# A mixture-of-experts loop regrouped into pairs of tiles, with six shared-expert units moved inside it

## What is computed

```python
logits = jnp.einsum('btc,ec->bte', x, router_w)          # 16 experts
top_vals, top_idx = jax.lax.top_k(logits, TOP_K)         # TOP_K = 2
gates = jax.nn.sigmoid(top_vals)
...
gu = jnp.einsum('nc,ech->neh', xf, gate_up_w)            # per expert, 128 -> 256
gate, up = jnp.split(gu, 2, axis=-1)
h = jax.nn.silu(gate) * up
out_all = jnp.einsum('neh,ehc->nec', h, down_w)          # per expert, 128 -> 128
moe = jnp.einsum('ne,nec->nc', w_full, out_all)
sg = jnp.einsum('btc,sc->bts', x, shared_gate_w)         # shared expert, for every row
su = jnp.einsum('btc,sc->bts', x, shared_up_w)
shared = jnp.einsum('bts,cs->btc', jax.nn.silu(sg) * su, shared_down_w)
return moe + shared
```

## Time and profile before

| | |
|---|---|
| median of 3 runs | 781.0 us (776.43 to 783.17) |
| the profiled execution, its own time | 782.83 us |
| its span, first to last instruction | 780.8 us |
| PE busy | 591.2 us (76%) |
| DVE busy | 495.7 us (63%) |
| POOL busy | 330.2 us (42%) |
| ACT busy | 288.7 us (37%) |
| mean granted TensorE clock | 0.889 of full |

### The profile page before, as it was taken

How to read it: one execution, slowest core, us unless ns; L and a number is a source line. 1 busy time by engine, 2 the same in 40 slices (tenths; PEclk the granted TensorE clock), 3 DMA queues, 4 the chain that set the end, 5 groups by cost and what they waited for, 6 DMA issues and landing times. The chain is left out here.

```text
span 780.8 us, 17864 instructions
## 1 busy us (share of the span) xinstructions
PE 591.2 (76%) x5275; PEld 392.6 (50%) x5276; DVE 495.7 (63%) x1390; ACT 288.7 (37%) x812; POOL 330.2 (42%) x628
## 2 busy tenths in 40 slices
PE   4775888888888888778778887875667876777772
PEld 3554666566665665344434444453335654655441
DVE  8564677886778766689798888874422332232367
ACT  2523444454444542144333434432223433343110
POOL 7531333323233231116565766765424544454100
PEclk9976999999999998699889889987877897797997
DMA  5785344335433533513231322320222222222343
GB/s 156 119 286 77 77 78 60 73 78 83 68 60 72 79 75 73 135 47 81 62 95 52 96 61 74 82 68 17 91 56 69 75 72 76 67 82 64 122 121 94
DMA packets 95331, 65.85 MB, mean 84 GB/s; under 512 B 24752, under 2 KB 90624, under 8 KB 95296
## 3 DMA queue, kind: packets, MB, share of 16 engines
q1 hardware_dynamic: 90688, 55.44, 31.7%
q0 software_dynamic: 4608, 9.97, 4.0%
HBM read 20.54 MB, written 17.56 MB: 49 GB/s over the span
## 5 line engine op out<-in xcount | busy, mean ns | idle before, releaser
L573 POOL DMA_INDIRECT expert_out<-ey,xt x80 | 77.5, 969 | 91.7 <-DVE ey L878 74.8
L968 ACT ACTIVATE probs<-ps 128x512 f32<-128x512 f32 x128 | 73.1, 596 | 64.0 <-PE ps L1364 31.9
L630 DVE TENSOR_REDUCE nmax<-ps 128x8 f32<-128x512 f32 x128 | 81.2, 683 | 19.4 <-PE ps L1226 11.8
L873 DVE TENSOR_TENSOR eh<-ps,sg 128x128 f32<-128x128 f32 x80 | 23.3, 291 | 105.2 <-ACT sg L1090 81.8
L549 POOL DMA_INDIRECT expert_in<-xn,sloti x64 | 64.5, 1008 | 27.4 <-issue 14.6
L1195 PE MATMUL ps<-probs,constants 128*32 128x256 f32 x512 | 72.5, 429 | 0.0
L649 DVE RECIPROCAL rden<-ps 128x256 f32<-128x256 f32 x32 | 56.2, 1756 | 21.4 <-PE ps L1195 16.1
L1457 PE MATMUL ps<-wgu,xtT 128*128 x160 | 66.6, 506 | 2.0 <-ACT xtT L1084 1.5
L442 POOL TENSOR_SCALAR veps<-mv 128x2 f32<-128x2 f32 x48 | 10.7, 224 | 119.5 <-issue 84.2
L1450 PE MATMUL ps<-constants,xt 128*128 128x128 f32 x80 | 27.9, 349 | 38.1 <-issue 22.0
L1364 PE MATMUL ps<-qs,ckbd 128*128 128x256 bf16 x128 | 25.9, 311 | 23.3 <-DVE qs L645 10.7
(11 more groups left out here) (207 smaller groups left out, 1442.8 us busy)
## 6 DMA issues: line engine op xcount, KB each, us to landing
qs<-part SPq DMA_DIRECT2D x192, 64.0 KB, 3.4
kbd<-part SPq DMA_DIRECT2D x96, 128.0 KB, 3.9
xt<-expert_in SPq DMA_DIRECT2D x80, 72.0 KB
ck_scr<-wgu SPq DMA_DIRECT2D x6, 512.0 KB, 4.5
ckbd<-ck_scr SPq DMA_DIRECT2D x16, 192.0 KB
expert_in<-zero_rows SPq DMA_DIRECT2D x32, 72.0 KB
wgu<-in_L_ffn_gate_up_w SPq DMA_DIRECT2D x1, 2048.0 KB, 9.6
cvbd<-cvbd_all SPq DMA_DIRECT2D x16, 128.0 KB
```

The lines of the kernel that those rows point to most:

```text
L573: pool.indirect_dma_start(ys, bass.IndirectOffsetOnAxis(xt[p][:, E:E + 1].bitcast(I32), 0), ey[p % 4][:, :], None).then_inc(e_(f"out{p % 4 ...
L630: v.tensor_reduce(nmax[:, u, 8 * half:8 * half + 8], bank[:, :].rearrange("p (h k) -> p h k", k=64), AX.X, ALU.max, negate=True).then_inc( ...
L968: a_.activation(probs[:, 2 * i:2 * i + 2, :], P2[i % 2][:, :].rearrange("p (j q) -> p j q", j=2), ACT.Exp, scale=SCALE).then_inc(s("probs" ...
```

## The change

The loop works on pairs of tiles, called steps here: `STEPS` = 40. A stage handles both tiles with one wait and one signal, and ACT and DVE instructions are twice as wide. The stages stand one, three and four steps behind the load: at step s PE turns the pair s and the `eh` pair s-3 into one bank (`turns`), multiplies the pair s-1 by the first weights (`gate_up`) and the pair s-4 by the second (`down`). One ACT copy takes both transposes. The ring `xt` has 16 tiles, `ey` four pairs.

A loop body holds eight steps, 16 tiles. The program is eight steps written out, three bodies in which six shared-expert units are mixed (one unit to four steps), one body without them, and four steps of rest on the engines that lag. At the head of each body SP reads 16 registers and PE 22; ahead of the first steps PE reads 14, and before the rest 8. `later_units` is gone. All 16 batches are combined at the end.

In a mixed group of four steps q = 0 to 3, each part stands behind the step's own work: PE `shared_in` at q = 0 and 1, `shared_out` at q = 3; ACT the silu at q = 0 and 1; DVE the addition of the unit before at q = 0 and the products at q = 1 and 2.

```diff
-RING = 8
+RING, BACK = 16, 8
...
+        EARLY = 2
+        MIXED = B // 2 - EARLY
+        TURNS = RING // 2
+        STEPS = TILES // 2
+        MIXES = MIXED // 2
+
+        def step_loop(eng, step, most, before=None, mixed=None):
+
+            if before:
+                before(0)
+            for s in range(TURNS):
+                step(s, 0, s)
+            with eng.Fori(1, MIXES + 1) as i:
                 if before:
                     before(i)
+                for q in range(TURNS):
+                    step(TURNS * i + q, i, q)
+                    if mixed:
+                        mixed(2 * i + EARLY - 2 + q // 4, q % 4)
+            with eng.Fori(MIXES + 1, STEPS // TURNS) as i:
...
+            def tiles_in(s, i, q):
+                wait_apart(sp, (e_("tt_ps"), s - 3 if not isinstance(s, int) or s > 3 else 0),
+                           *(((e_(f"out{q % 4}"), 32 * (2 * i + q // 4 - 1)),) if not isinstance(i, int) or i > 0 else ()))
+                for p in (2 * q, 2 * q + 1):
+                    sp.dma_start(xt[p][:, :], xs[bass.ds(first[p], 128), :]).then_inc(e_(f"in{q % 4}"), 16)
...
+                def rows_out(s, i, q):
+                    wait_apart(pool, (e_("y"), s + 1))
+                    for j in range(2):
+                        p = 2 * q + j
+                        pool.indirect_dma_start(ys, bass.IndirectOffsetOnAxis(xt[p][:, E:E + 1].bitcast(I32), 0),
+                                                ey[q % 4][:, j, :], None).then_inc(e_(f"out{q % 4}"), 16)
...
+                def mixed(u, q):
+                    if q == 0:
+                        shared_end(u - 1, SHARED_OUT)
+                    if q in (1, 2):
+                        shared_gated(u, q - 1, SHARED_IN[1])
...
-                later_units(shared, two_combined)
                 dve.wait_ge(h_("x"), B // 2)
-                for b in range(B - 2 * EARLY - 2, B):
+                for b in range(B):
                     combine(b)
...
+                def shared_in(u, c, banks):
+                    at_least(pe, h_("h"), 2 * u + c - (0 if banks is SHARED_IN else 1))
                     for k in range(2):
...
+                def mixed(u, q):
+                    if q in (0, 1):
+                        shared_in(u, q, SHARED_IN)
+                    if q == 3:
+                        shared_out(u, SHARED_OUT)
...
+                    where = i if isinstance(i, int) else 1
+                    tiles = range(-8 if where else 0, RING - 2 if where < STEPS // TURNS else 0)
+                    held = numbers(pe, tile_row[0:1, 1, bass.ds(RING * i + tiles[0], len(tiles))], NE - 1)
...
+                def turns(s, i, q):
+                    at_least(pe, e_("turned"), s - 1)
...
+                def gate_up(m, p, tile):
+                    pe.wait_ge(e_("turned"), m + 1)
+                    at_least(pe, e_("h"), m - 1)
...
+                def down(m, p, tile):
+                    pe.wait_ge(e_("turned"), m + 4)
+                    at_least(pe, e_("y"), m)
```

More of the change, by code:

```diff
@@ L244, in loop2, with due @@
                 body(n - 2 + k, n // 2 - 1, k)
[L246 to L257, removed]
+        EARLY = 2
[9 more added lines that the diff above has]
+            with eng.Fori(1, MIXES + 1) as i:
                 if before:
                     before(i)
[L260 to L272, removed]
+                for q in range(TURNS):
[3 more added lines that the diff above has]
+            with eng.Fori(MIXES + 1, STEPS // TURNS) as i:
+                if before:
+                    before(i)
+                for q in range(TURNS):
+                    step(TURNS * i + q, i, q)
+            if most and before:
+                before(STEPS // TURNS)
+            for s in range(STEPS, STEPS + most):
+                step(s, s // TURNS, s % TURNS)
+        def due(m):
+            return not isinstance(m, int) or 0 <= m < STEPS
         def loop(eng, body, alone=2):
@@ L424, in _ @@
                 sp.wait_ge(e_(f"out{q}"), 16 * (TILES // 4))
-            for b in range(RING):
+            for b in range(BACK):
                 rows_back(b)
@@ new lines, in silu, with step @@
+                def silu(m, p):
+                    act.wait_ge(e_("gu_ps"), m + 1)
+                    at_least(act, e_("h"), m - 1)
+                    gates = GU[p][:, :].rearrange("p (j h) -> p j h", j=2)[:, :, 0:ED]
+                    a_.activation(sg[p][:, :, :], gates, ACT.Silu).then_inc(e_("silu"), 1)
+                def step(s, i, q):
+                    if due(s) or due(s - 3):
+                        copy(s, q % 2)
+                    if due(s - 1):
+                        silu(s - 1, (q + 1) % 2)
@@ L1103, in _ @@
+                def mixed(u, q):
+                    if q in (0, 1):
+                        shared_silu(u, q, SHARED_IN[0])
+                step_loop(act, step, 3, None, mixed)
         @block.tensor
@@ L1472, in _ @@
-                skewed(pe, [(turn, 0), (gate_up, 1), (turn_h, 2), (down, 3)], TILES, load_experts)
-                pe.wait_ge(e_("y"), TILES)
-                later_units(shared)
+                    where = i if isinstance(i, int) else 1
+                    tiles = range(-8 if where else 0, RING - 2 if where < STEPS // TURNS else 0)
+                    held = numbers(pe, tile_row[0:1, 1, bass.ds(RING * i + tiles[0], len(tiles))], NE - 1)
+                    expert.clear()
+                    expert.update(zip(tiles, held))
@@ new lines, in gate_up @@
+                def gate_up(m, p, tile):
+                    pe.wait_ge(e_("turned"), m + 1)
+                    at_least(pe, e_("h"), m - 1)
+                    for j in range(2):
+                        last = mm(GU[p][:, 2 * ED * j:2 * ED * j + 2 * ED], turned[p][:, 128 * j:128 * j + 128],
+                                  wgu[:, bass.ds(expert[tile + j], 1), :].squeeze(1), start=True, stop=True)
+                    last.then_inc(e_("gu_ps"), 1)
+                def down(m, p, tile):
+                    pe.wait_ge(e_("turned"), m + 4)
+                    at_least(pe, e_("y"), m)
+                    for j in range(2):
+                        last = mm(YT[:, E * j:E * j + E], turned[p][:, 256 + 128 * j:384 + 128 * j],
+                                  wd[:, bass.ds(expert[tile + j], 1), :].squeeze(1), start=True, stop=True)
+                    last.then_inc(e_("y_ps"), 1)
@@ L1478, with step @@
+                def step(s, i, q):
+                    if due(s) or due(s - 3):
+                        turns(s, i, q)
+                    if due(s - 1):
+                        gate_up(s - 1, (q + 1) % 2, 2 * q - 2)
+                    if due(s - 4):
+                        down(s - 4, (q + 1) % 2, 2 * q - 8)
+                step_loop(pe, step, 4, load_experts, mixed)
 W_LOADS, W_LATER = 6, 19
```

199 lines of the change are left out of this document (83 added, 116 removed).

## The result

The changed kernel took 747.2 us (median of 4, 744.77 to 750.47), the one before 781.4 (median of 4, 776.43 to 783.17): a ratio of 0.9575, 95% interval 0.9517 to 0.9632, so 4.3% faster where 1.9% was forecast. The profiled execution took 750.47 us, its span 748.6, against 780.8 before. All ratios here are taken from executions in the same, faster state, and one execution of b1_read_even at 1211 us is left out of its ratio.

The account below looks back on a forecast made before the run. No engine was full; the write-to-load circle and PE's register reads with low clock bound the loop. Filling to 585.9, heads and mixed bodies to 703.6, last write landing 739.0, tail 26.8: span 765.8, forecast 766 us, range 736 to 782.

Parts of the forecast that it names:

- the read at the heads: At each mixed body's head and the last's, PE's read of 22 numbers takes 5.5 us; pauses 5.5 once, 4.4 three times.
- rival 1: PE's register read is nearly a fixed cost, 22 numbers in 1.0 us, hidden behind `shared_out`: 738 us, chance 0.33.
- The clock behind a head: After each long read pause PE runs 5.6 us at half speed, costing 2.8 us each.
- The rate of a read: PE's register reads cost 0.247 us per further number; the page's rate at one end of its own range, 755 to 779.
- A pair's time on PE: In the loop a pair of tiles streams through PE in 2.08 us at full clock, 3.42 low.
- The wait at q = 1: In mixed groups PE waits 1.3 us ahead of `shared_in` for DVE's product, twice a body; other waits are covered.
- The ring: In the loop the load's round trip takes 8.3 us against POOL's 10.2 for eight DMAs, so it no longer binds.
- The last body: Without shared units POOL binds, 24 DMAs at 1.27 us; the last begins at 736.7 and lands at 739.0.
- The tail: All 16 batches combined after the last write: 26.8 us, with 3.2 until a batch lands, and no waits for reads back.
- the end of the filling: PE ends the first eight steps at 585.9 us in the forecast, at 585.4 in rival 1.
- Rivals 2 and 3: Clock stays low in mixed bodies, 823 us, chance 0.08; steps slowed by waits counted as covered, no change, 781 us, 0.09.

Follow-up runs that it names:

- b1_read_even: The kernel before, but PE's read at each body head takes 12 numbers from 8i - 4 in place of 10 from 8i - 3: 768.2 us, 0.9882 of before.
- a1_read_odd: The changed kernel, but PE's head reads begin one number earlier, 23 numbers from 16i - 9 in place of 22 from 16i - 8: 765.0 us, 0.9859 of before.
- a2_dve_first: The changed kernel, but DVE does the shared products of q = 1 and 2 ahead of the step's own work: 742.1 us, 0.9557 of before.
- d1_own_places: The changed kernel, but DVE copies each pair's places aside, so loads wait for the eviction and not the write: 751.6 us, 0.9609 of before.
- c runs: Four on one chip: changed kernel unaltered, 733.3 us; with reads of 24, 736.1; with ACT and DVE written out, 737.1; both with DVE's shared products first, 721.6.
- c0_changed: The changed kernel, unaltered, measured again on another chip: 733.3 us, 0.953 of before.
- d3_three_again: The changed kernel with DVE's shared products first, ACT and DVE written out and reads of 24, run again on another chip: 739.1 us, 0.9452 of before.

## Why the prediction was right in direction and wrong in size

**The step that failed is the read at the heads**: "For 22 numbers PE's two rows give 0.305 + 21 x 0.247 = 5.5 us", and the choice behind it, "I take 5.5, since it comes from the same engine, the same array and a read of more than eight". It measured 1.88. The sentence under rival 1 named the true condition, where the read starts, and the forecast then gave the wrong side the larger chance. All of the old PE reads of more than one number began three numbers ahead of a multiple of eight; SP's row of 8 in 0.52 us was the one read that began on a multiple, as all the new ones do. Among the rows at hand the likeness in start counted, not the engine. a1_read_odd is the forecast's own world: with a read of 5.8 us the ratio was 0.986, and the forecast's 766 for 781 is 0.981; with the read of 1.88 it is 0.9575. That the forecast comes so near a1_read_odd is partly luck, since errors of both signs stand beside the read in the table. The read explains the 13.1 us of the pauses in the table, and most of the clock's part, next. The other half of that term held: forecast, the sequencer hides 1.1 us of a read behind `shared_out`; measured, 1.92 us of read made a pause of 0.69, and 5.82 one of 4.57 in a1_read_odd, so 1.2 are hidden.

**The clock behind a head** was priced at 2.8 us each, 5.6 us at half speed, and hung on the length of the pause. Half speed was a granted clock of 0.50 in the kernel before. Its loop had ten such stretches, five of about 3.4 us and five of about 6.8, 5.7 a body (an estimate from windows of 1 us); one of them, 601.1 to 607.9, began within the pause of 2.73 us and holds the tiles at 1.71 us. Pauses of 0.7 us left the granted clock at 1.00 [windows above]; the one of 3.93 us was followed by 0.50 from 592.7 to 596.2 and by a body at 0.94, 1.7 us longer than the other two. In place of 8.4 us the low clock cost 1.7. The mechanism holds for the long pause. Its price was 1.7 and not 2.8, as behind the long pauses of a1_read_odd (1.5 to 1.7), and behind the other heads there was nothing to pay.

**The rate of a read** at the lower end of the forecast's own range is shown by no run. Where the read begins on a multiple of four, 22 numbers in 1.88 us are 85 ns each and 24 in 1.65 are 69. Where it doesn't, 23 numbers in 5.76 us are 250 ns each.

**A pair's time on PE**, 2.08 us by columns, measured 1.75. I had doubled the old tile of 1.04 us whole. By the starts of PE's matmuls `gate_up` takes 0.43 us a tile in both kernels. What shrank is the share of the `eh` transpose (0.18 us a tile to 0.11) and that of `down` (0.32 to 0.23). That these were waits or hand-overs, which a pair has once and two tiles twice, is likely but not shown: PE counts as busy through all of the 1.04. Over 24 mixed steps that is 7.9 us, of which 5.7 show in the table, the rest taken by the waits at q = 1 (1.5 us for the 1.3 forecast, 1.2 us in six) and small ones.

**The wait at q = 1** stood in the one place forecast and nowhere else in a mixed group, and a2_dve_first removed it by the cause given.

**The ring**: "The ring no longer binds; POOL does where PE has only experts" failed. It bound at the first head, where the load of step 8 waits for the write of pair 0. The forecast had priced that wait at nothing. Its terms from the eviction to the transposes (0.42, 2.25, 1.27, 0.7 and 1.57) make 6.2 us; measured were 8.8 (583.08 to 591.91). The write began 0.8 us after the eviction's end, which was not counted, the second half landed 3.0 us after its start and not 2.25, and SP's two issues took 2.0 us and not 0.7 (588.6 to 590.65). The wait of 3.40 us at 693.12 has the same circle, 8.35 us long, but what set it off came before. The eviction that began it stood on DVE behind a product that waited for ACT, and ACT had come 2.7 us late to its copy at 683.52. POOL was idle for 3.28 us ahead of the write, so no queue of writes was in the way:

```profile
684.77 0.42 DVE L895 COPY ey<-ps 128x256 f32<-128x256 f32 x1
...
685.94 0.97 POOL L580 DMA_INDIRECT expert_out<-ey,xt  x1 [3.28 <-DVE ey L895]
```

With the loads freed (d1_own_places) the last body took as long, through the second circle by way of PSUM, ACT and DVE.

**The last body**, forecast 33.1 us, took 39.5 in the trace above, but 33.4 to 34.6 in the four c runs. There the waits for loads are present too (0.20, 0.84 and 1.94 us in c0_changed), and ACT's pauses are not. So the forecast's POOL-bound 33.1 was near where ACT answers at once, and the 6.4 us over it go in the main with ACT's pauses, whose cause is open. They are not all of it: in a1_read_odd, with 38.6 us, ACT's pauses are short, and PE waits 4.10 us for one load.

**The tail**: forecast 29.05 from the last write's start, measured 28.87, with no wait in the combines. The reads back landed after 5.0 us in the median, not 3.2, and the eight batches ahead hid it, as the sum had counted.

**The rivals**: rival 1, 738 us, had the read nearly right (1.0 us for 1.88, and no low clock behind it). It still missed, by 9 us on the median and 10.7 on the span: 4.3 at the loop's start, in code not touched, 4.6 in the pauses at the heads, 3.9 of them the load at the first, and 7.7 in the last body (39.5 for 31.8), against shorter steps. Its 585.4 for the end of the filling doesn't follow from its own read either: with 14 numbers in 0.8 us the first load would have bound, and the filling would have ended near 584.8. Rivals 2 and 3 didn't happen.

**What stays open** is why the last body and its rest take 33 us in one profile and 40 in another with the same code. In the four c runs each silu of that stretch starts 0.03 to 0.6 us after PE's product for it. In the long ones ACT comes late to inputs that PE has ready, at the longest 1.2 us in a1_read_odd and 2.7 to 3.6 in the others, and POOL gets gaps of 2 to 3.5 us. Writing ACT's program out did not remove it (d3_three_again). The trace puts the end of some of these pauses down to PE and of others to a signal that it can't name (`remote`), so it doesn't say what ACT waits for. ACT's timeline in d3_three_again, where PE had finished the inputs of these two silus at about 684.3 and 694.4, by its matmuls' times (L1500):

```profile
687.04 0.38 ACT L1120 ACTIVATE sg<-ps 128x256 f32<-128x256 f32 x1 [2.30 <-remote]
...
697.52 0.38 ACT L1120 ACTIVATE sg<-ps 128x256 f32<-128x256 f32 x1 [2.41 <-remote]
```

One transfer of an instruction queue falls into such a pause in d1_own_places (692.0 to 692.5, ACT idle until 693.50), but in c0_changed one at 672.2 has no such pause behind it. No run here takes these transfers away, so their part is not shown.

## What to carry to other kernels

Before a duration is scaled by its count, ask in what the rows at hand are alike with the new case: here two rows differed in engine, count and alignment at once, and the one read off an odd start was taken as the law. When the price of a step carries others on its back (the pause that lowers the clock), it deserves a two-line run of its own, or at least an equal chance for the other value. And an edit that is to remove a pause says nothing where the kernel beside it doesn't have the pause: look at the neighbour's trace on the same chip first. A ring's round trip is to be counted with every hop between engines in it, and from an eviction as late as the engines ahead of it can make it: when a freed buffer makes a wait vanish, the next circle may stand right behind it, here one PSUM bank evicted behind a later pair's product.

## What the runs showed of the hardware

A register read of 22 or 24 numbers that starts on a multiple of four took 1.88 and 1.65 us on PE (12 took 0.86, 8 took 0.61), one of 23 that starts off it 5.76 (10 took 2.53, 9 took 2.30). On such a multiple 24 numbers took 0.79 us more than 12, 0.07 a number; off it 23 took 3.23 us more than 10, 0.25 a number. From the same starts, more numbers took less time in two cases: 24 for 22, above, and the first read of the program, 1.30 us for 16 and 1.54 for 14. Why is not shown. For reads of more than one number on PE, the starts that were run are multiples of four, three ahead of a multiple of eight, and one ahead of one. SP's were faster by the number, 16 in 1.0 us and 8 in 0.52.

Row writes that follow each other without a gap started every 1.27 to 1.28 us in every run, whatever the kernel, and those on the chains that ended last landed 2.2 to 3.7 us after their start.

The same kernel took 747 us in the first measurement and 733 on the chip of the c runs, where the kernel before also took less (769 for 781 us). In the last body ACT came late to ready inputs in the six other profiles of the mixed loop and in none of the four on this chip.
